# A selective-scan layer and an expert layer on one core: the delta stage keeps its exponentials in SBUF, in place, and gives the PSUM banks to products and projections

## The chip, the core and the metric

The kernel runs on one core of a Trainium2 chip. Time is the device time of one execution in microseconds (us), the median of several runs. The core's engines run side by side, each its own program in order: TensorE (PE, matrix products; PEld is its weight load), VectorE (DVE) and GpSimd (POOL) for element-wise work, ScalarE (ACT) for functions such as exp and log, and SyncE (SP), which here only issues DMAs. They wait for each other by semaphores. Products land in PSUM, which has eight banks of 128 partitions x 512 fp32; everything else lies in SBUF.

## What is computed

Two layers. In the first, the image x (2 x 256 x 48 x 48) is normalized and cut into 8 units (2 images x 4 branches of 64 channels). Each unit goes through this:

```python
x = silu(depthwise_conv3x3(x @ in_W) + conv_b)                  # 128 channels, L = 2304 positions
xs = stack([x, x_transposed, x[::-1], x_transposed[::-1]])      # K = 4 directions
dts, Bmat, Cmat = split(einsum('bkdl,kcd->bkcl', xs, x_proj_W)) # R = 4, N = 16, N = 16 rows
delta = softplus(einsum('bkrl,kdr->bkdl', dts, dt_W) + dt_b)
# scan over L: h = h * exp(delta * A) + (delta * u) * B ; y = sum_n h * C
```

then a norm, an output product and a skip. The second layer is an attention over all 4608 positions and a mixture of 8 experts. The part that matters here is softplus(v), which the kernel computes as max(v, 0) + log(1 + exp(-|v|)) with a correction for what is lost when 1 is added to the exponential.

## The kernel before

The program is a row of stages: setup, norm, delta, scan, mid (the join of the four directions, and the output product), attention, blend, gate, experts. Each stage ends before the next begins.

The delta stage writes delta and delta * u for the scan, and the rows B and C. Its loop has 16 groups: group g is unit g // 2 and the pair of directions g % 2, so 2 x 2304 = 4608 columns, cut into nine pieces (i = 0 to 8) of 512 columns. n = 9 g + i numbers the pieces. Each engine's program is written out by hand; its order is the order of the loops in the code:

- TensorE, per piece: `expand` (the product with dt_W in two matmuls, high and low part, into a bank of `ps_a`), in six of the nine pieces `project` (384 columns of the rows for the group to come, into `ps_b`), and half a block of the convolution for a unit to come (`convolve`, into `ps_c`). `expand` waits until the bank's last reader, the third VectorE operation, is done (`v_done`). `project` waits until the block before it has been taken out of `ps_b` (`lo_done`, `even_taken`).
- ScalarE, per piece: `magnitude(n + 1)`, the absolute value of the product, from `ps_a` to the SBUF buffer `mag`; then the exponential of piece n, from `mag` to a bank of `ps_e`, which waits until VectorE is done with that bank (`co_done`); then, where there is a projection, one or two copies out of `ps_b` (`take_block`). After nine pieces come three logarithms of 1536 columns each (`log`), in place in `du`, the third of which needs VectorE's second operation of piece 8. Exponentials after logarithms need a table load, and so do logarithms after exponentials. After the even groups a SiLU of the next unit follows (`silu`), but for the last unit.
- VectorE, per piece: first (L541) `du` = (e + 1) - 1, second (L545) `de` = e - `du`, third (L549) `de` = max(v, 0) + `de`, v still in `ps_a`. Between first and second stands `take_block`: a copy of 96 rows (every second block) and the low part of the rows to be cut. Between second and third stands, in pieces 1, 4 and 7, the copy of a convolution block out of `ps_c` (`take_conv`).
- GpSimd, after the logarithms of a group: six additions (`add_log`, L564) and six products (`drive`, L571) of 768 columns, alternately. After each even group it also makes the transposed image of the next unit (`turn`, L557).
- SyncE stores each part of 768 columns as it is done.

PSUM's eight banks are three for `ps_a`, two for `ps_e`, one for `ps_b`, two for `ps_c`.

Of the kernel before, what the change touches and what calls it, by code (L numbers as in the profile page):

```python
# [276 lines left out]
def delta_phase(nc, P, keep):  # L277
# [4 lines left out]
    with ExitStack() as ctx:  # L282
# [3 lines left out]
        xt = [s.sb(f"xt{i}", [128, L]) for i in range(2)]  # L286
        bc = [s.sb(f"bc{i}", [6 * N, L]) for i in range(2)]
        cut = [s.sb(f"cut{i}", [STACK, L], F32R) for i in range(2)]
        mag = [s.sb(f"mag{i}", [128, PIECE]) for i in range(3)]
        de = [s.sb(f"de{i}", [128, 2 * L]) for i in range(2)]  # L290
        du = [s.sb(f"du{i}", [128, 2 * L]) for i in range(2)]
        ps_a = [s.ps(f"ps_a{i}", [128, PIECE]) for i in range(3)]
        ps_e = [s.ps(f"ps_e{i}", [128, PIECE]) for i in range(2)]
        ps_b = s.ps("ps_b", [128, PIECE])
        ps_c = [s.ps(f"ps_c{i}", [128, PIECE]) for i in range(2)]
        cleared, ones_set, xs_ready, xt_ready = s.sem("cleared"), s.sem("ones_set"), s.sem("xs_ready"), s.sem("xt_ready")
        img_here = [s.sem(f"img_here{i}") for i in range(2)]
# [90 lines left out]
        @block.tensor  # L388
        def _(pe):
            def convolve(unit, t, first, last):  # L390
                o = ps_c[t % 2][:, 0:TT]
                ov = o.rearrange("p (r w) -> p r w", w=W)
                iv = img[unit % 2][:, :].rearrange("p (r w) -> p r w", w=W)
                r0 = t * (TT // W)
                RB = TT // W
                if first == 0:
                    if t == 0:
                        pe.wait_ge(img_here[unit % 2], 32 * (unit // 2) + 32)
                    if unit * TPI + t >= 2:
# [12 lines left out]

            def project(g, b):
                u, p = divmod(g, PAIRS)
                m = TPI * g + b
                if b == 0:
                    if p == 0:
                        pe.wait_ge(xs_ready, u + 1)
                    else:
                        pe.wait_ge(xt_ready, u + 1)  # L420
                if m:
                    pe.wait_ge(lo_done, m)
                    pe.wait_ge(even_taken, (m + 1) // 2)
                x = xs[u % 3] if p == 0 else xt[u % 2]
                pe.matmul(ps_b[:, 0:TT], keep["w_bc"][:, p, :], x[:, b * TT:b * TT + TT], start=True, stop=True).then_inc(b_full, 1)

            def expand(g, i):
                n = g * IG + i
                pe.wait_ge(hi_done, TPI * g + blocks_for(i))
                pe.wait_ge(lo_done, TPI * g + blocks_for(i))  # L430
                if n >= 3:
                    pe.wait_ge(v_done, n - 2)
                for r, at, a, b in spans(i):
                    d = g % PAIRS + 2 * r
                    pe.matmul(ps_a[n % 3][:, a:b], keep["w_dt"][:, d, :], cut[g % 2][:, at:at + b - a], start=True, stop=False)
                    mm = pe.matmul(ps_a[n % 3][:, a:b], keep["w_dt_lo"][:, d, :], cut[g % 2][:, at:at + b - a], start=False, stop=True)
                mm.then_inc(a_full, 1)

            for t in range(TPI):
                convolve(0, t, 0, 6)  # L440
            for t in range(3):
                convolve(1, t, 0, 6)
            pe.wait_ge(ones_set, 2)
            for b in range(TPI):
                project(0, b)
            for g in range(G):
                for i in range(IG):
                    expand(g, i)
                    if proj_block(g, i):
                        project(*proj_block(g, i))  # L450
                    if conv_block(g, i) and i % 3 < 2:
                        convolve(*conv_block(g, i), 3 * (i % 3), 3 * (i % 3) + 3)

        @block.scalar
        def _(act):
# [4 lines left out]
            def take_block(g, b):  # L460
# [3 lines left out]
                    act.wait_ge(bc_out[g % 2], 128 * (g // 2))  # L464
                    act.wait_ge(a_full, IG * (g - 1))
                if m % 2 == 0:
                    act.activation(bc[g % 2][:, b * TT:b * TT + TT], ps_b[0:6 * N, 0:TT], ACT.Copy).then_inc(even_taken, 1)
                act.activation(cut[g % 2][0:40, b * TT:b * TT + TT], ps_b[0:40, 0:TT], ACT.Copy).then_inc(hi_done, 1)

            def magnitude(n):  # L470
                act.wait_ge(a_full, n + 1)
                act.activation(mag[n % 3][:, :], ps_a[n % 3][:, :], ACT.Abs).then_inc(mag_done, 1)

            def log(g, r):
                act.wait_ge(co_done, IG * g + 3 * r + 3)
# [8 lines left out]
            for g in range(G):  # L484
                for i in range(IG):
# [1 line left out]
                    if n + 1 < G * IG:  # L487
                        magnitude(n + 1)
                    act.wait_ge(mag_done, n + 1)
                    if n >= 2:  # L490
                        act.wait_ge(co_done, n - 1)
                    act.activation(ps_e[n % 2][:, :], mag[n % 3][:, :], ACT.Exp, scale=-1.0).then_inc(ex_done, 1)
                    if i + 1 < IG and proj_block(g, i + 1):
                        take_block(*proj_block(g, i + 1))
                for r in range(LOGS):
# [5 lines left out]
        def _(dve):  # L501
# [8 lines left out]
            def take_block(g, b):  # L510
                m = TPI * g + b
                dve.wait_ge(hi_done, m + 1)
                if m % 2:
                    dve.tensor_copy(bc[g % 2][:, b * TT:b * TT + TT], ps_b[0:6 * N, 0:TT]).then_inc(odd_taken, 1)
                at = slice(b * TT, b * TT + TT)
                dve.tensor_tensor(cut[g % 2][64:104, at], ps_b[0:40, 0:TT], cut[g % 2][0:40, at].bitcast(F32), ALU.subtract).then_inc(lo_done, 1)

            for k in range(2):
                dve.memset(img[k][:, :], 0.0)
            for k in range(2):  # L520
                dve.memset(cut[k][64:STACK, :].bitcast(F32), 0.0)
                dve.memset(cut[k][32:64, :].bitcast(F32), 1.0).then_inc(ones_set, 1)
# [9 lines left out]
            for g in range(G):  # L532
                for i in range(IG):
# [16 lines left out]

        @block.gpsimd
        def _(pool):
# [1687 lines left out]
```

## Time and profile before

| | us |
|---|---|
| median of 3 runs | 5893.06 |
| lowest, highest | 5884.61, 5897.52 |
| the profiled execution | 5879.69 |
| its span, first to last instruction | 5877.3 |
| of it the delta stage's loop, 176 to 681 us | 505 |

The profile is of one execution. Its times count from the span's start. A row of the timeline says when an instruction started, how long it took, the engine, the line of the code, what it wrote from what it read, and in brackets how long its engine had stood idle before it and for whose result. Rows that follow each other directly on one engine are merged, with their number (x2). A group of the table by line has the number of instructions, their busy time and the mean of one, then the idle time of the engine just before them. Instructions on one engine overlap by about 0.1 us where they need nothing of each other, so their starts tell their pace better than their durations. Names are those of the code with the stage ahead: delta_ps_a is `ps_a` of the delta stage.

### The profile page before, as it was taken

To read this page: it belongs to the slowest core of one execution; us is meant where nothing else is said; L and a number is where in the kernel's file an instruction comes from. 1 tells how busy PE (TensorE), PEld (TensorE's weight loads), DVE (VectorE), ACT (ScalarE), POOL (GpSimd) and SP (SyncE) were. 2 spreads that over 40 slices of the span, in tenths; PEclk is the share of its full clock that TensorE was granted. 3 is DMA by queue.
4 is the path that set the end of the run, shared out by engine and by line. 5 is a ranking of instruction groups with operands and counts; after the bars stand their busy time and mean duration, and the time that the engine had idled before them with its cause. 6 is when DMAs were issued, how large, how long until landed. Compare 5 with 4: busy or idle time off the path is not lost. (4 is left out here: it accounts for less than half of the span.)

```text
span 5877.3 us, 82874 instructions
## 1 busy us (share of the span) xinstructions
PE 5051.9 (86%) x21540; PEld 3367.2 (57%) x21540; DVE 4209.1 (72%) x4029; ACT 3787.9 (64%) x8376; POOL 4259.4 (72%) x2720
## 2 busy tenths in 40 slices
PE   4777499999899898898898889995799999995997
PEld 2344255555555555555555555553458888884675
DVE  3677599999999999999999999996751111118334
ACT  2566588888888888888888888883442222226332
POOL 0576699999999999999999999995504444444442
PEclk8889599999999999999999999998999999996898
DMA  3676677777777777777777777775600000004113
GB/s 91 172 212 208 207 241 248 248 249 250 242 252 247 238 248 246 246 245 240 248 245 241 247 249 248 248 250 193 229 26 0 0 0 0 0 0 123 50 58 132
DMA packets 395504, 1045.37 MB, mean 178 GB/s; under 512 B 53422, under 2 KB 90319, under 8 KB 390944
## 3 DMA queue, kind: packets, MB, share of 16 engines
q1 hardware_dynamic: 380816, 1009.75, 53.0%
q0 software_dynamic: 7584, 20.72, 1.0%
q10 hardware_dynamic: 6640, 9.74, 0.4%
q8 instruction: 166, 2.72, 0.2%
q14 instruction: 298, 2.44, 0.1%
HBM read 869.23 MB, written 170.79 MB: 177 GB/s over the span
## 5 line engine op out<-in xcount | busy, mean ns | idle before, releaser
L909 POOL TENSOR_TENSOR scan_hc<-scan_h,scan_c_rep 128x768 f32<-128x768 f32 x1536 | 2749.3, 1822 | 227.3 <-PE scan_ps_y L740 180.2
L740 PE MATMUL scan_ps_y<-scan_hc,keep_ident 128*128 128x512 f32 (+1 forms) x6144 | 2217.6, 489 | 23.6 <-ACT scan_y L775 23.2
L874 DVE TENSOR_TENSOR_SCAN scan_h<-scan_da,scan_h,scan_ps_p 128x768 f32<-128x768 f32 x896 | 1568.6, 1796 | 0.0
L740 PEld LDWEIGHTS scan_ps_y<-scan_hc,keep_ident 128*128 128x128 f32 x6144 | 1066.6, 190 | 823.1 <-issue 738.1
L792 ACT ACTIVATE scan_warm<-scan_du_t 128x128 f32<-128x128 f32 x4608 | 1423.6, 388 | 35.8 <-PE scan_ps_p L731 30.2
L831 ACT ACTIVATE scan_da<-scan_dd,layer_a_neg 128x768 f32<-128x768 f32 x1344 | 1184.7, 922 | 6.1 <-issue 5.7
L1456 POOL TENSOR_TENSOR attn_e_lo<-attn_e,attn_e_hi 128x512 fp32r<-128x512 f32 x324 | 420.2, 1297 | 605.1 <-DVE attn_e_hi L1447 605.1
L731 PE MATMUL scan_ps_p<-keep_ident,scan_warm 128*128 128x128 f32 x4608 | 646.7, 277 | 224.2 <-DVE scan_h L874 223.4
L874 DVE TENSOR_TENSOR_SCAN scan_h<-scan_da,scan_ps_p 128x768 f32<-128x768 f32 x448 | 758.8, 1735 | 2.2 <-ACT scan_da L831 2.0
L731 PEld LDWEIGHTS scan_ps_p<-keep_ident,scan_warm 128*128 128x128 f32 x4608 | 531.9, 141 | 374.3 <-issue 157.0
L853 DVE TENSOR_TENSOR scan_ps_p<-scan_ps_p,scan_dd 128x768 f32<-128x768 f32 x576 | 547.5, 951 | 186.1 <-PE scan_ps_p L723 185.2
L1447 DVE CAST attn_e_hi<-attn_e 128x512 fp32r<-128x512 f32 x324 | 146.4, 452 | 721.5 <-ACT attn_e L1435 721.5
L1435 ACT ACTIVATE attn_e<-attn_ps_s 128x512 f32<-128x512 f32 x324 | 194.0, 599 | 705.8 <-PE attn_ps_s L74 705.8
L723 PE MATMUL scan_ps_p<-scan_cut,layer_b_sel 128*128 128x512 f32 (+1 forms) x1152 | 381.1, 412 | 56.9 <-DVE scan_h L874 48.7
L831 ACT ACTIVATE scan_ps_p<-scan_dd,layer_a_neg 128x768 f32<-128x768 f32 x192 | 172.2, 897 | 273.8 <-DVE scan_h L874 273.8
L903 POOL TENSOR_TENSOR scan_bu<-scan_dd,scan_b_rep 128x768 f32<-128x768 f32 x192 | 348.4, 1814 | 0.0
L564 POOL TENSOR_TENSOR delta_de<-delta_de,delta_du 128x768 f32<-128x768 f32 x96 | 173.5, 1814 | 182.5 <-ACT delta_du L477 182.5
L723 PEld LDWEIGHTS scan_ps_p<-scan_cut,layer_b_sel 128*128 128x128 f32 x1152 | 196.0, 190 | 155.9 <-DVE scan_h L874 134.6
L72 PE MATMUL attn_ps_o<-attn_e_hi,t_lo 128*128 128x512 f32 x648 | 259.6, 401 | 0.0
L72 PE MATMUL attn_ps_s<-f_hi,f_lo 128*128 x648 | 255.1, 394 | 2.1 <-DVE t_lo L1443 2.1
L74 PE MATMUL attn_ps_o<-attn_e_hi,t_hi 128*128 128x512 f32 x648 | 256.8, 396 | 0.0
L73 PE MATMUL attn_ps_s<-f_lo,f_hi 128*128 x648 | 255.8, 395 | 0.0
(328 smaller groups left out, 6869.4 us busy)
## 6 DMA issues: line engine op xcount, KB each, us to landing
scan_c_rep<-bc_dram SPq DMA_DIRECT2D x1536, 384.0 KB, 4.1
scan_dd<-dd_dram SPq DMA_DIRECT2D x96, 768.0 KB, 5.7
scan_b_rep<-bc_dram SPq DMA_DIRECT2D x192, 384.0 KB, 4.7
dd_dram<-delta_de SPq DMA_DIRECT2D x96, 384.0 KB, 2.6
dd_dram<-delta_du SPq DMA_DIRECT2D x96, 384.0 KB, 3.2
y_dram<-scan_y SPq DMA_DIRECT2D x96, 384.0 KB, 4.4
mid_nat<-y_dram SPq DMA_DIRECT2D x48, 384.0 KB, 5.3
delta_img<-xn_dram SPq DMA_DIRECT2D x16, 576.0 KB, 8.6
```

The costliest lines, as they stand in the source:

```text
L72: pe.matmul(out, wl, xh, start=start, stop=False)
L74: return pe.matmul(out, wh, xh, start=False, stop=stop)
L723: mm = pe.matmul(ps_p[place(t) % PR][:, lo:hi], keep["b_sel"][:, n, :], cut[st % 2][:, lo:hi], start=True, stop=True)
L731: mm = pe.transpose(ps_p[place(t) % PR][:, b * 128:b * 128 + 128], warm[w % WR][:, b, :], keep["ident"][:, :])
L740: mm = pe.matmul(ps_y[:, lo:hi], keep["ident"][:, :], hc[t % HR][:, lo:hi], start=n == 0, stop=n == N - 1)
L792: last = act.activation(warm[w % WR][:, b, :], du_t[st % 2][:, b * 128:b * 128 + 128], ACT.Identity, scale=du_t[st % 2][:, at:at + 1])
L831: act.activation(dst, dd[st % 2][:, 0, :], ACT.Exp, scale=keep["a_neg"][:, k, n:n + 1]).then_inc(ex_done, 1)
L853: dve.tensor_tensor(x, x, dd[st % 2][:, 1, :], ALU.mult).then_inc(mult_done, 1)
L874: dve.tensor_tensor_scan(view(h[n]), view(x), view(y), start, ALU.mult, ALU.add).then_inc(scan_done, 1)
L903: pool.tensor_tensor(bu[f % SR][:, :], dd[st % 2][:, 1, :], b_rep[f % SR][:, :], ALU.mult).then_inc(bu_done, 1)
L909: pool.tensor_tensor(hc[t % HR][:, :], h[t % N][:, :], c_rep[t % CR][:, :], ALU.mult).then_inc(hc_done, 1)
L1456: pool.tensor_tensor(e_lo[j % 3][:, :], e[j % 3][:, :], e_hi[j % 3][:, :].bitcast(F32), ALU.subtract).then_inc(lo_done, 1)
```

## The change

Three edits, all in the delta stage:

1. The exponential is written over its argument in `mag`, which has six buffers in place of three; `ps_e` is gone. `magnitude` waits for the buffer (`co_done`, six pieces back), the exponential waits for nothing but its argument. VectorE's first two operations read `mag`. The first becomes a `scalar_tensor_tensor`, whose second operand is a new column `less` of -1, broadcast over 512 columns.
2. The two banks go to a fourth buffer of `ps_a` and a second of `ps_b`. `expand` waits for the piece four back, `project` for the block two back.
3. `take_conv` stands in pieces 2, 5 and 8.

```diff
-        mag = [s.sb(f"mag{i}", [128, PIECE]) for i in range(3)]
+        MR, AR = 6, 4
+        mag = [s.sb(f"mag{i}", [128, PIECE]) for i in range(MR)]
+        less = s.sb("less", [128, 1])
...
-        ps_a = [s.ps(f"ps_a{i}", [128, PIECE]) for i in range(3)]
-        ps_e = [s.ps(f"ps_e{i}", [128, PIECE]) for i in range(2)]
-        ps_b = s.ps("ps_b", [128, PIECE])
+        ps_a = [s.ps(f"ps_a{i}", [128, PIECE]) for i in range(AR)]
+        ps_b = [s.ps(f"ps_b{i}", [128, PIECE]) for i in range(2)]
...
-                if m:
-                    pe.wait_ge(lo_done, m)
-                    pe.wait_ge(even_taken, (m + 1) // 2)
+                if m >= 2:
+                    pe.wait_ge(lo_done, m - 1)
+                    pe.wait_ge(even_taken, m // 2)
...
-                if n >= 3:
-                    pe.wait_ge(v_done, n - 2)
+                if n >= AR:
+                    pe.wait_ge(v_done, n - AR + 1)
...
-                act.activation(mag[n % 3][:, :], ps_a[n % 3][:, :], ACT.Abs).then_inc(mag_done, 1)
+                if n >= MR:
+                    act.wait_ge(co_done, n - MR + 1)
+                act.activation(mag[n % MR][:, :], ps_a[n % AR][:, :], ACT.Abs).then_inc(mag_done, 1)
...
-                    if n >= 2:
-                        act.wait_ge(co_done, n - 1)
-                    act.activation(ps_e[n % 2][:, :], mag[n % 3][:, :], ACT.Exp, scale=-1.0).then_inc(ex_done, 1)
+                    act.activation(mag[n % MR][:, :], mag[n % MR][:, :], ACT.Exp, scale=-1.0).then_inc(ex_done, 1)
...
+            dve.memset(less[:, :], -1.0)
...
-                    dve.tensor_scalar(du[g % 2][:, at], ps_e[n % 2][:, :], 1.0, -1.0, ALU.add, ALU.add).then_inc(dm_done, 1)
+                    dve.scalar_tensor_tensor(du[g % 2][:, at], mag[n % MR][:, :], 1.0, less[:, 0:1].to_broadcast([128, PIECE]), ALU.add, ALU.add).then_inc(dm_done, 1)
...
-                    dve.tensor_tensor(de[g % 2][:, at], ps_e[n % 2][:, :], du[g % 2][:, at], ALU.subtract).then_inc(co_done, 1)
-                    if conv_block(g, i) and i % 3 == 1:
+                    dve.tensor_tensor(de[g % 2][:, at], mag[n % MR][:, :], du[g % 2][:, at], ALU.subtract).then_inc(co_done, 1)
+                    if conv_block(g, i) and i % 3 == 2:
                         take_conv(*conv_block(g, i))
                     dve.wait_ge(co_done, n + 1)
-                    dve.scalar_tensor_tensor(de[g % 2][:, at], ps_a[n % 3][:, :], 0.0, de[g % 2][:, at], ALU.max, ALU.add).then_inc(v_done, 1)
+                    dve.scalar_tensor_tensor(de[g % 2][:, at], ps_a[n % AR][:, :], 0.0, de[g % 2][:, at], ALU.max, ALU.add).then_inc(v_done, 1)
```

VectorE at the end of the first group, pieces 7 and 8 and the first operation of the next group; before:

```order
L541 TENSOR_SCALAR delta_du0<-delta_ps_e1 128x512 [waits delta_ex_done]
L514 COPY delta_bc1<-delta_ps_b 96x384 [waits delta_hi_done]
L516 TENSOR_TENSOR delta_cut1<-delta_ps_b,delta_cut1 40x384
L545 TENSOR_TENSOR delta_de0<-delta_ps_e1,delta_du0 128x512 [waits delta_dm_done]
L508 COPY delta_xs1<-delta_ps_c1 128x384 [waits delta_c_full]
L549 SCALAR_TENSOR_TENSOR delta_de0<-delta_ps_a1,delta_de0 128x512 [waits delta_co_done]
L541 TENSOR_SCALAR delta_du0<-delta_ps_e0 128x512 [waits delta_ex_done]
L545 TENSOR_TENSOR delta_de0<-delta_ps_e0,delta_du0 128x512 [waits delta_dm_done]
L549 SCALAR_TENSOR_TENSOR delta_de0<-delta_ps_a2,delta_de0 128x512 [waits delta_co_done]
L541 TENSOR_SCALAR delta_du1<-delta_ps_e1 128x512 [waits delta_ex_done]
```

The same place now:

```order
L543 SCALAR_TENSOR_TENSOR delta_du0<-delta_mag1,delta_less 128x512 [waits delta_ex_done]
L515 COPY delta_bc1<-delta_ps_b1 96x384 [waits delta_hi_done]
L517 TENSOR_TENSOR delta_cut1<-delta_ps_b1,delta_cut1 40x384
L547 TENSOR_TENSOR delta_de0<-delta_mag1,delta_du0 128x512 [waits delta_dm_done]
L551 SCALAR_TENSOR_TENSOR delta_de0<-delta_ps_a3,delta_de0 128x512 [waits delta_co_done]
L543 SCALAR_TENSOR_TENSOR delta_du0<-delta_mag2,delta_less 128x512 [waits delta_ex_done]
L547 TENSOR_TENSOR delta_de0<-delta_mag2,delta_du0 128x512 [waits delta_dm_done]
L509 COPY delta_xs1<-delta_ps_c1 128x384 [waits delta_c_full]
L551 SCALAR_TENSOR_TENSOR delta_de0<-delta_ps_a0,delta_de0 128x512 [waits delta_co_done]
L543 SCALAR_TENSOR_TENSOR delta_du1<-delta_mag3,delta_less 128x512 [waits delta_ex_done]
```

The convolution copy moved from piece 7 to piece 8, behind the operation that counts up `co_done`; the first two operations of each piece have two operands in SBUF.

ScalarE at the same place, from the last block copy over the logarithms to the next group's first exponential; before:

```order
L468 ACTIVATE delta_cut1<-delta_ps_b 40x384 [waits delta_b_full]
L472 ACTIVATE delta_mag0<-delta_ps_a0 128x512 [waits delta_a_full]
L492 ACTIVATE delta_ps_e0<-delta_mag2 128x512 [waits delta_co_done,delta_mag_done]
L477 ACT_TABLE_LOAD
L477 ACTIVATE delta_du0<-delta_du0 128x1536 [waits delta_co_done] x3
L458 ACT_TABLE_LOAD
L458 ACTIVATE delta_xs1<-delta_xs1,layer0_conv_b 128x2304 [waits delta_c_taken]
L472 ACTIVATE delta_mag1<-delta_ps_a1 128x512 [waits delta_a_full]
L492 ACT_TABLE_LOAD [waits delta_co_done]
L492 ACTIVATE delta_ps_e1<-delta_mag0 128x512 [waits delta_mag_done]
```

And now:

```order
L469 ACTIVATE delta_cut1<-delta_ps_b1 40x384 [waits delta_b_full]
L475 ACTIVATE delta_mag3<-delta_ps_a1 128x512 [waits delta_co_done,delta_a_full]
L493 ACTIVATE delta_mag2<-delta_mag2 128x512 [waits delta_mag_done]
L480 ACT_TABLE_LOAD
L480 ACTIVATE delta_du0<-delta_du0 128x1536 [waits delta_co_done] x3
L459 ACT_TABLE_LOAD
L459 ACTIVATE delta_xs1<-delta_xs1,layer0_conv_b 128x2304 [waits delta_c_taken]
L475 ACTIVATE delta_mag4<-delta_ps_a2 128x512 [waits delta_co_done,delta_a_full]
L493 ACT_TABLE_LOAD
L493 ACTIVATE delta_mag3<-delta_mag3 128x512 [waits delta_mag_done]
```

The order of ScalarE's work is as it was; the wait for `co_done` moved from the exponential to the magnitude.

## Rows read from the trace of the kernel before

**Rows 1.** Windows: each engine's busy us (instructions), TensorE's clock, DMA share, GB/s

```profile
176.00:681.00 505.00, 341.21 (x950) 187.99 (x948) 378.63 (x606) 337.63 (x513) 349.84 (x188) 0.83 0.69 205
```

**Rows 2.** Groups by line, VectorE, 176 to 681 us: busy, mean ns | idle before, releasers

```profile
L545 DVE TENSOR_TENSOR delta_de<-delta_ps_e,delta_du 128x512 f32<-128x512 f32 x144 | 99.6, 692 | 4.7
...
L541 DVE TENSOR_SCALAR delta_du<-delta_ps_e 128x512 f32<-128x512 f32 x144 | 99.0, 687 | 116.4 <-ACT delta_ps_e L492 115.8
```

**Rows 3.** Waits, 176 to 681 us: us in total, times, longest

```profile
POOL delta_de L564 <- ACT delta_du L477: 182.5, 16, 51.7
```

**Rows 4.** Timeline around two group ends: start, us, engine, line [idle before]

```profile
393.27 4.23 ACT L477 ACTIVATE delta_du<-delta_du 128x1536 f32<-128x1536 f32 x3
...
403.53 0.69 DVE L541 TENSOR_SCALAR delta_du<-delta_ps_e 128x512 f32<-128x512 f32 x1 [7.70 <-ACT delta_ps_e L492]
...
423.29 0.69 DVE L549 SCALAR_TENSOR_TENSOR delta_de<-delta_ps_a,delta_de 128x512 f32<-128x512 f32 x1
...
424.26 0.69 DVE L541 TENSOR_SCALAR delta_du<-delta_ps_e 128x512 f32<-128x512 f32 x1 [0.28 <-ACT delta_ps_e L492]
...
424.87 0.54 DVE L514 COPY delta_bc<-delta_ps_b 96x384 f32<-96x384 f32 x1
...
426.03 0.69 DVE L545 TENSOR_TENSOR delta_de<-delta_ps_e,delta_du 128x512 f32<-128x512 f32 x1
...
427.10 0.68 DVE L549 SCALAR_TENSOR_TENSOR delta_de<-delta_ps_a,delta_de 128x512 f32<-128x512 f32 x1
427.26 4.23 ACT L477 ACTIVATE delta_du<-delta_du 128x1536 f32<-128x1536 f32 x3
427.70 0.68 DVE L541 TENSOR_SCALAR delta_du<-delta_ps_e 128x512 f32<-128x512 f32 x1
...
428.41 0.69 DVE L545 TENSOR_TENSOR delta_de<-delta_ps_e,delta_du 128x512 f32<-128x512 f32 x1
...
428.82 3.61 POOL L564 TENSOR_TENSOR delta_de<-delta_de,delta_du 128x768 f32<-128x768 f32 x2 [8.55 <-ACT delta_du L477]
...
432.38 1.81 POOL L571 TENSOR_TENSOR delta_du<-delta_de,delta_xt 128x768 f32<-128x768 f32 x1
...
433.99 0.69 DVE L541 TENSOR_SCALAR delta_du<-delta_ps_e 128x512 f32<-128x512 f32 x1 [4.16 <-ACT delta_ps_e L492]
...
458.11 4.23 ACT L477 ACTIVATE delta_du<-delta_du 128x1536 f32<-128x1536 f32 x3
```

**Rows 5.** Timeline in the mid stage, VectorE and GpSimd

```profile
4127.72 2.79 POOL L1030 TENSOR_TENSOR mid_q<-f_lo 128x768 f32<-128x768 f32 x1
4127.79 3.53 DVE L1269 SCALAR_TENSOR_TENSOR mid_a<-mid_nat,mid_d_sum,mid_a 128x768 f32<-128x768 f32 x1 [1.70 <-POOL mid_a L1025]
4130.47 2.52 POOL L1025 TENSOR_TENSOR mid_a<-mid_nat 128x768 f32<-128x768 f32 x1
4131.36 2.44 DVE L1273 TENSOR_TENSOR mid_a<-mid_a,mid_q 128x768 f32<-128x768 f32 x1
4132.95 3.51 POOL L1030 TENSOR_TENSOR mid_q<-f_lo 128x768 f32<-128x768 f32 x1
```

**Rows 6.** Timeline in the gate stage, VectorE and GpSimd

```profile
5415.19 2.61 POOL L1792 TENSOR_TENSOR keep_w_lo<-gate_raw,keep_w_hi 128x1024 fp32r<-128x1024 f32 x1 [2.21 <-ACT keep_w_hi L1821]
5415.52 3.10 DVE L1916 TENSOR_TENSOR gate_hot_r<-keep_iota,gate_rt 128x768 bf16<-128x768 f32 x1
```

**Rows 7.** Lines L239 and L243, norm stage: times, min/median/max ns, first and last start

```profile
L239 DVE TENSOR_TENSOR norm_xc<-norm_x,norm_ps_m x12: 953/954/955, 32.0 to 71.7; 128x768 f32<-128x768 f32 x12
...
L243 DVE TENSOR_TENSOR norm_xc<-norm_xc,norm_rs x12: 951/952/959, 47.4 to 84.8; 128x768 f32<-128x768 f32 x12
```

**Rows 8.** Line L557, delta stage

```profile
L557 POOL COPY delta_xt<-delta_xs x8: 4127/4179/4227, 144.5 to 610.6; 128x2304 f32<-128x2304 f32 x8
```

**Rows 9.** Timeline of the first group's row blocks, first projection and last cut

```profile
152.87 0.81 PE L425 MATMUL delta_ps_b<-delta_xs,layer_w_bc 128*128 128x384 f32 x2
...
170.13 0.55 DVE L516 TENSOR_TENSOR delta_cut<-delta_ps_b,delta_cut 40x384 fp32r<-40x384 f32 x1
```

More of the change, by code:

```diff
@@ L420, in project @@
                         pe.wait_ge(xt_ready, u + 1)
-                if m:
-                    pe.wait_ge(lo_done, m)
-                    pe.wait_ge(even_taken, (m + 1) // 2)
+                if m >= 2:
+                    pe.wait_ge(lo_done, m - 1)
+                    pe.wait_ge(even_taken, m // 2)
                 x = xs[u % 3] if p == 0 else xt[u % 2]
-                pe.matmul(ps_b[:, 0:TT], keep["w_bc"][:, p, :], x[:, b * TT:b * TT + TT], start=True, stop=True).then_inc(b_full, 1)
+                pe.matmul(ps_b[m % 2][:, 0:TT], keep["w_bc"][:, p, :], x[:, b * TT:b * TT + TT], start=True, stop=True).then_inc(b_full, 1)
             def expand(g, i):
@@ L430, in expand @@
                 pe.wait_ge(lo_done, TPI * g + blocks_for(i))
-                if n >= 3:
-                    pe.wait_ge(v_done, n - 2)
+                if n >= AR:
+                    pe.wait_ge(v_done, n - AR + 1)
                 for r, at, a, b in spans(i):
                     d = g % PAIRS + 2 * r
-                    pe.matmul(ps_a[n % 3][:, a:b], keep["w_dt"][:, d, :], cut[g % 2][:, at:at + b - a], start=True, stop=False)
-                    mm = pe.matmul(ps_a[n % 3][:, a:b], keep["w_dt_lo"][:, d, :], cut[g % 2][:, at:at + b - a], start=False, stop=True)
+                    pe.matmul(ps_a[n % AR][:, a:b], keep["w_dt"][:, d, :], cut[g % 2][:, at:at + b - a], start=True, stop=False)
+                    mm = pe.matmul(ps_a[n % AR][:, a:b], keep["w_dt_lo"][:, d, :], cut[g % 2][:, at:at + b - a], start=False, stop=True)
                 mm.then_inc(a_full, 1)
@@ L466, in take_block @@
                 if m % 2 == 0:
-                    act.activation(bc[g % 2][:, b * TT:b * TT + TT], ps_b[0:6 * N, 0:TT], ACT.Copy).then_inc(even_taken, 1)
-                act.activation(cut[g % 2][0:40, b * TT:b * TT + TT], ps_b[0:40, 0:TT], ACT.Copy).then_inc(hi_done, 1)
+                    act.activation(bc[g % 2][:, b * TT:b * TT + TT], ps_b[m % 2][0:6 * N, 0:TT], ACT.Copy).then_inc(even_taken, 1)
+                act.activation(cut[g % 2][0:40, b * TT:b * TT + TT], ps_b[m % 2][0:40, 0:TT], ACT.Copy).then_inc(hi_done, 1)
             def magnitude(n):
                 act.wait_ge(a_full, n + 1)
-                act.activation(mag[n % 3][:, :], ps_a[n % 3][:, :], ACT.Abs).then_inc(mag_done, 1)
+                if n >= MR:
+                    act.wait_ge(co_done, n - MR + 1)
+                act.activation(mag[n % MR][:, :], ps_a[n % AR][:, :], ACT.Abs).then_inc(mag_done, 1)
             def log(g, r):
@@ L513, in take_block @@
                 if m % 2:
-                    dve.tensor_copy(bc[g % 2][:, b * TT:b * TT + TT], ps_b[0:6 * N, 0:TT]).then_inc(odd_taken, 1)
+                    dve.tensor_copy(bc[g % 2][:, b * TT:b * TT + TT], ps_b[m % 2][0:6 * N, 0:TT]).then_inc(odd_taken, 1)
                 at = slice(b * TT, b * TT + TT)
-                dve.tensor_tensor(cut[g % 2][64:104, at], ps_b[0:40, 0:TT], cut[g % 2][0:40, at].bitcast(F32), ALU.subtract).then_inc(lo_done, 1)
+                dve.tensor_tensor(cut[g % 2][64:104, at], ps_b[m % 2][0:40, 0:TT], cut[g % 2][0:40, at].bitcast(F32), ALU.subtract).then_inc(lo_done, 1)
             for k in range(2):
                 dve.memset(img[k][:, :], 0.0)
+            dve.memset(less[:, :], -1.0)
             for k in range(2):
```

## The prediction

> **What bounds the kernel now.** I read the windows by stage first: the change touches only the delta stage, whose main loop is a stretch of 505 us in which VectorE works 379 us, GpSimd 350, TensorE 341 and ScalarE 338 [rows 1]. No engine is full, so the stage is a chain. The groups of VectorE's lines say where it breaks: 115.8 us of idle time stand in front of the first operation of a piece, until ScalarE's exponential [rows 2]. The timeline shows the shape of it [rows 4]. A group is nine pieces of 512 columns. At its end ScalarE does three logarithms with a table load before and after them, and then the first exponential of the next group; VectorE has finished its last piece and stands for 4.16 us, or 7.70 us where a SiLU comes in between as well. Two groups, one with the SiLU and one without, take 458.11 - 393.27 = 64.84 us. In between VectorE runs at its own pace, with 0.28 us lost now and then. GpSimd has its twelve operations of 1.8 us after each set of logarithms, and is idle 182.5 us in all, 51.7 of them before its first [rows 3]. So the stage is bound by VectorE plus the stand at each group's end, with GpSimd working beside VectorE for about 23 of each 32 us.
>
> **What the change gains.** Pieces of VectorE, from the starts in [rows 4]: first operation to second 0.71 us (427.70 to 428.41), each row copy or cut between them 0.58 (424.87 to 426.03 holds two) in front of a first operation that then takes 0.61; third operation to the next piece 0.60; second to third 0.72, or 1.07 with a convolution copy. So a piece costs 2.5 us with one block operation, 3.1 with two, 2.05 with none, and 0.35 more with the copy: 8.0 for three, as before and after, since the copy moves from the second piece of three to the third. The one change there is that the copy of piece 8 stands behind the operation that the logarithm waits for.
> Fourth product buffer: before, the logarithms start at 427.26, 3.28 us after the third operation of piece 6 ends (423.29 + 0.69); that is the expansion for the next group, its magnitude, the exponential of piece 8 and the table load. With four buffers and exponentials that need no bank, the same chain hangs on piece 5. Counted from the start of piece 6 (time 0), the logarithms then start at 0.1 + 3.3 = 3.4. Two logarithms end at 6.3; the third needs the second operation of piece 8, which without any disturbance starts at 2.5 + 3.1 + 0.7 = 6.3 and ends at 7.0. The third logarithm ends at 8.5. From the end of the logarithms to the next group's first operation the rows give 433.99 - 431.49 = 2.5 us, and 403.53 - 397.50 = 6.0 us with the SiLU: 11.0 and 14.5. Six more pieces of 16.0 together: 27.0 and 30.5, with some 0.8 of TensorE's delay behind the SiLU left in, 58.4 us for two groups where there were 64.8. Over seven such pairs and one more boundary that is about 47 us.
> Second projection bank: the first six row blocks take from 152.87 to 170.68 [rows 9], one after another, since each projection waits for the cut of the block before it. Two banks let two blocks overlap; of nearly 3 us a block I take 1.5 off for four of them: 6 us (0 to 8). In the loop projections are not late, so nothing there.
> New memset, one column: nothing. ScalarE writes SBUF in place of PSUM: ScalarE has at least 2 us to spare per piece once VectorE is late; nothing, and at the group's end one exponential, within 0.1 us a group either way.
> VectorE's sources: SBUF in place of PSUM. The same form of 768 columns took 954 ns with one PSUM source and 952 ns with two SBUF sources [rows 7], GpSimd idle both times: nothing. The Trainium skill ("VectorE: DVE Perf Modes", the section on the TRN2 errata) has 58 cycles for SBUF and 120 for PSUM; that would be 62 cycles less, an estimate of 0.065 us for each of 288 operations, 19 us. The rows don't show it, and it is not in the sum.
>
> **What the change costs.** It gives two of VectorE's three operations per piece two SBUF inputs: the first now reads the exponentials and a broadcast column, the second the exponentials and the result of the first. Before, each had one input in PSUM, and with GpSimd beside them they kept to 692 and 687 ns [rows 2]. The trace has VectorE operations with two SBUF inputs beside GpSimd in the stage that joins the scans [rows 5]. At 4127.79 such an operation of 768 columns takes 3.53 us; GpSimd's began at 4127.72 and ended at 4130.51, and VectorE's ends 0.81 later. GpSimd's next took 2.52, not 1.81, and VectorE's next ends again 0.8 after it (4131.36 + 2.44 = 4133.80). So it is one after the other: VectorE's operation waits for the whole GpSimd operation, then goes first, and GpSimd's next is put off by 0.71. A broadcast operand does not help: in [rows 6] an operation whose second operand is a broadcast takes 3.10 us, until 0.82 after GpSimd's end at 5417.80.
> The Trainium skill says so too ("SBUF — State Buffer", Who interferes with whom): a VectorE instruction with two SBUF inputs contends with a GpSimd one that reads SBUF, and the later of the two is blocked for all of it. By that rule, the trace agrees, in every pair in [rows 5].
> For 512 columns I take 0.26 us off, the difference between 954 ns for 768 columns [rows 7] and 692 ns for 512 [rows 2]: VectorE's operation ends 0.55 after GpSimd's, and GpSimd is put off 0.45. GpSimd alone has a cadence of 1.77 ((432.38 - 428.82) / 2). So under GpSimd one of these operations goes through per 1.77 + 0.45 = 2.22 us. What VectorE does between them (0.6 to 1.3 us) fits into that; a piece takes 4.4 us for 2.7. The walk, from the start of piece 6:
> GpSimd starts 1.56 after the logarithms (428.82 - 427.26), at 5.0. The first operation of piece 8 asks at 5.6, waits for 6.8, ends 7.3; the second waits for GpSimd's next, until 9.0, and ends 9.55 in place of 7.0. Third logarithm until 11.0; next group at 13.5, or 17.05 with the SiLU. GpSimd's operations 3 to 7 run at 1.77 from 9.4 on and end at 11.2, 13.0, 14.7, 16.5, 18.3.
> Without SiLU: blocked operations go at the ends of GpSimd's 5 to 12, the first at 14.7 and the last at 14.7 + 7 x 2.22 = 30.2. These are eight, so four pieces; piece 4 starts at 31.4, and 3.1 + 2.4 later piece 6: 36.9.
> With SiLU: operations 7 to 12 carry six, 18.3 to 29.4; then GpSimd's turn, a copy of 4.18 us [rows 8], holds the first operation of piece 3 until 34.0, and piece 6 starts at 41.9. Before, the pair was 64.84; now 78.8: 14.0 more. Seven pairs are 98, the one odd boundary 6.5: +104. The gains of the first part are inside the walk. Less 6 for the first blocks: **+98 us**.
> The profiled execution took 5879.7 us (span 5877.3 and 2.4 around it): 5977.7. The median of the runs stands 13.4 above it, so I forecast **5990**.
> Where I chose: that the turn blocks like the two-input operations is not in the rows; without it the seven SiLU groups lose 2.9 us less, 20 in all. The first blocked operation of piece 8 is only 0.6 us later than GpSimd's start; were it earlier, 1.2 us a group go, 17 in all. And 0.1 us on each of about 140 blocked operations is 14. Together with the 0 to 8 us of the first blocks these give 5945 to 6010.
>
> **Rivals.**
> (a) Nothing blocks: the broadcast and the in-place buffers are read as PSUM was. Then the first part stands alone, -47 and -6: **5840**, faster. It speaks for it that [rows 2] show both lines at an even 690 ns beside GpSimd; against it that there each has only one SBUF input, and that [rows 5, 6] show the wait for both forms. It would decide from a wait below a third of what I take: the gain is 53, the blocking costs 151. 7 in 100.
> (b) Only the second operation blocks, the broadcast being free. The same walk, with one blocked operation a piece: 30.4 and 36.2, pair 66.6, +12 over seven pairs, less 6: **5900**, the same. Against it [rows 6]. 5 in 100.
> (c) GpSimd does not give way after each operation, or not always. Then VectorE's pieces come nearly all after GpSimd's: 5 + 12 x 1.77 + six pieces of 16 us is 42 to 43 for 36.9 without the SiLU, +6 per group: **6080**. Against it the alternation in [rows 5], where VectorE goes first at every end of a GpSimd operation. 6 in 100.
> (d) The blocking is as walked, but the stand behind it grows, since the stores or TensorE come late by it: up to 6040. Part of the main case's range.
>
> **How the numbers follow.** The walk has 82 in 100, of which 4 lie below 5945 or above 6040; (a) 7, (b) 5, (c) 6. The range 5945 to 6040 holds about 8 in 10. A measurement here tells 0.2%, 12 us. Faster is (a): 0.07. Same: (b), 0.05. Slower: 0.88.
>
> **What the profile after would show.** Right: the two lines that write delta_du and delta_de from delta_mag have a minimum near 690 ns and a mean well above, 1.3 to 1.5 us, with maxima near 2.4 and 4.7; the third, with its PSUM input, stays at 690; GpSimd's adds and products rise from 1.81 to a mean near 2.1; two groups take near 79 us from logarithm to logarithm. The idle time before the first operation of a piece falls below 80 us, and the stage is slower all the same. The scan and later stages don't change. Wrong: both lines at 690 and pairs of 58 us (a); the first line at 690 alone (b); single waits of several GpSimd operations (c). If the pair is 79 but the total isn't, a later stage gave or took it.

## The result, and the profile after

The changed kernel takes 5983.74 us (median of 4 runs, 5979.22 to 5989.98), the kernel before 5895.29 us (5884.61 to 5898.23): a ratio of 1.0151, 95% interval 1.0133 to 1.0169, so 88 us slower (78 to 100). The profiled execution took 5984.46 us, its span is 5982.6.

The windows by stage: each engine's busy us (instructions), TensorE's clock, DMA share, GB/s. This is the loop of the delta stage after; [rows 1] answer to it.

```profile
165.00:774.00 609.00, 365.83 (x951) 203.09 (x950) 526.54 (x604) 338.74 (x513) 406.25 (x188) 0.77 0.58 170
```

The loop takes 609 us where it took 505, for nearly the same instructions (604 of VectorE's for 606). VectorE's busy time grew from 379 to 527 us, GpSimd's from 350 to 406; ScalarE's did not move. The groups by line in the delta stage after, VectorE and GpSimd: shape, count | busy us, mean ns | idle before, releaser. [Rows 2] answer to the first two.

```profile
L543 DVE SCALAR_TENSOR_TENSOR delta_du<-delta_mag,delta_less 128x512 f32<-128x512 f32 x144 | 182.6, 1268 | 74.8 <-ACT delta_mag L493 74.8
L547 DVE TENSOR_TENSOR delta_de<-delta_mag,delta_du 128x512 f32<-128x512 f32 x144 | 174.7, 1213 | 4.7
L551 DVE SCALAR_TENSOR_TENSOR delta_de<-delta_ps_a,delta_de 128x512 f32<-128x512 f32 x144 | 99.0, 688 | 3.6
```

```profile
L566 POOL TENSOR_TENSOR delta_de<-delta_de,delta_du 128x768 f32<-128x768 f32 x96 | 197.3, 2062 | 219.2 <-ACT delta_du L480 219.2
L573 POOL TENSOR_TENSOR delta_du<-delta_de,delta_xt 128x768 f32<-128x768 f32 x48 | 102.7, 2147 | 0.0
```

The two operations that now have both inputs in SBUF went from 687 and 692 ns to 1268 and 1213; the third, which reads PSUM and SBUF as before, is at 688. The idle time in front of a piece fell from 115.8 us to 74.8, as the change meant it to, and the stage is slower all the same. The blocked time stands in the rows as busy time, not as a wait: (1268 - 687 + 1213 - 692) ns x 144 = 159 us.

The timeline at the group end with a SiLU that begins at 422.61, VectorE, GpSimd and ScalarE: start, us, engine, line.

```profile
422.61 2.86 ACT L480 ACTIVATE delta_du<-delta_du 128x1536 f32<-128x1536 f32 x2
...
424.17 4.02 POOL L566 TENSOR_TENSOR delta_de<-delta_de,delta_du 128x768 f32<-128x768 f32 x2 [11.63 <-ACT delta_du L480]
...
424.94 1.59 DVE L543 SCALAR_TENSOR_TENSOR delta_du<-delta_mag,delta_less 128x512 f32<-128x512 f32 x1
...
426.56 2.17 DVE L547 TENSOR_TENSOR delta_de<-delta_mag,delta_du 128x512 f32<-128x512 f32 x1
...
428.77 1.48 ACT L480 ACTIVATE delta_du<-delta_du 128x1536 f32<-128x1536 f32 x1 [3.30 <-DVE delta_de L547]
...
436.31 1.70 DVE L543 SCALAR_TENSOR_TENSOR delta_du<-delta_mag,delta_less 128x512 f32<-128x512 f32 x1 [6.51 <-ACT delta_mag L493]
...
446.96 2.17 DVE L547 TENSOR_TENSOR delta_de<-delta_mag,delta_du 128x512 f32<-128x512 f32 x1
...
448.54 4.63 POOL L559 COPY delta_xt<-delta_xs 128x2304 f32<-128x2304 f32 x1
...
450.13 3.59 DVE L543 SCALAR_TENSOR_TENSOR delta_du<-delta_mag,delta_less 128x512 f32<-128x512 f32 x1
...
455.67 0.68 DVE L543 SCALAR_TENSOR_TENSOR delta_du<-delta_mag,delta_less 128x512 f32<-128x512 f32 x1
```

Both operations of piece 8 wait for one GpSimd operation each (1.59 and 2.17 us in place of 0.69), and the third logarithm waits 3.30 us for the second of them. At 450.13 VectorE waits for the whole of GpSimd's transposing copy. As soon as GpSimd is through, the operation takes 0.68 us again (455.67). The first logarithms after, at the two ends of one pair of groups and between its two groups; [rows 4] hold the pair of before:

```profile
264.04 2.86 ACT L480 ACTIVATE delta_du<-delta_du 128x1536 f32<-128x1536 f32 x2
...
305.99 2.86 ACT L480 ACTIVATE delta_du<-delta_du 128x1536 f32<-128x1536 f32 x2
...
342.96 2.86 ACT L480 ACTIVATE delta_du<-delta_du 128x1536 f32<-128x1536 f32 x2
```

78.9 us for two groups, where it was 64.84: 42.0 for the one with the SiLU and 37.0 for the one without. The scan's first instruction on VectorE comes at 815.1 us, 95.4 later than before; the rest of the program differs by 10 us between the two profiled executions, and over the profiled executions of all kernels here the scan's stretch varies by 16 us without a pattern.

### The profile page after: what moved, and what is told of

The parts are those of the page before. It is cut to its first block and busy times, and to the rows that moved or that the text cites. A ratio compares the mean times of both kernels' runs of the same rounds, so it can differ in the third digit from the quotient of the medians.

```text
span 5982.6 us, 82870 instructions
## 1 busy us (share of the span) xinstructions
PE 5076.2 (85%) x21540; PEld 3384.3 (57%) x21540; DVE 4364.9 (73%) x4030; ACT 3788.8 (63%) x8376; POOL 4319.2 (72%) x2720
## 5 line engine op out<-in xcount | busy, mean ns | idle before, releaser
L566 POOL TENSOR_TENSOR delta_de<-delta_de,delta_du 128x768 f32<-128x768 f32 x96 | 197.3, 2062 | 219.2 <-ACT delta_du L480 219.2
```

## The experiments

Each ratio is to runs of the kernel before on the same chip.

**1. Both operations with a PSUM input.** Everything as changed, but the operands are where GpSimd's reads don't meet them. The formula is another (maxima for sums), so only the time is read.

```diff
-  dve.scalar_tensor_tensor(du[..], mag[n % MR][:, :], 1.0, less[:, 0:1].to_broadcast([128, PIECE]), ALU.add, ALU.add)
+  dve.scalar_tensor_tensor(du[..], mag[n % MR][:, :], 1.0, ps_a[n % AR][:, :], ALU.add, ALU.max)
-  dve.tensor_tensor(de[..], mag[n % MR][:, :], du[..], ALU.subtract)
+  dve.tensor_tensor(de[..], ps_a[n % AR][:, :], du[..], ALU.max)
```

> The changed kernel, but the first two operations of VectorE's piece read the product bank ps_a in place of the column of -1 and in place of the exponentials, so that each has one SBUF input; buffers, waits and GpSimd's work are as changed (the formula is another: maxima in place of the sums). Theory (blocking behind GpSimd): both operations go back to an even 690 ns, GpSimd to 1.81 us, two groups take near 58.4 us from logarithm to logarithm, the total is near 5838 us (before 5895, less 47 for the groups and the 10.6 us by which the first group began earlier in the changed kernel). Rival (the slowdown comes from the buffers, the waits or ScalarE's writes to SBUF): two groups stay at 79 us and the total near 5984.

Measured: 5832.92 us, ratio 0.9902 (0.9874 to 0.9929). The groups by line of this kernel:

```profile
L547 DVE TENSOR_TENSOR delta_de<-delta_ps_a,delta_du 128x512 f32<-128x512 f32 x144 | 99.6, 692 | 4.7
L551 DVE SCALAR_TENSOR_TENSOR delta_de<-delta_ps_a,delta_de 128x512 f32<-128x512 f32 x144 | 99.2, 689 | 3.6
L543 DVE SCALAR_TENSOR_TENSOR delta_du<-delta_mag,delta_ps_a 128x512 f32<-128x512 f32 x144 | 97.8, 679 | 82.3 <-ACT delta_mag L493 82.3
```

Both are back at 690 ns, with GpSimd's additions at 1818 ns, and two groups take 59.2 to 60.3 us. So the whole loss is where the operands lie: 151 us between this kernel and the changed one. The rest of the change (the banks, the buffers, the moved copy) gains 61 us by the medians. Between the profiled executions it is 51, since that of before was one of the fastest of its kernel (see experiments 9 and 10).

**2 and 3. One operation at a time.** Only the first line of the diff above (with a maximum in the second operation), then only the second; what is computed differs in both, the work doesn't.

> The changed kernel, but only the first operation of the piece has a PSUM operand (ps_a for the column of -1, the formula is another); the second still has two SBUF inputs. Theory (each operation with two SBUF inputs waits for the GpSimd operation that runs): one blocked operation a piece, two groups near 66.6 us by the walk of the prediction's rival (b), the total near 5897; the first line at 690 ns, the second well above. Rival (only the broadcast column blocks): near 5838.

> The changed kernel, but only the second operation has a PSUM operand (ps_a for the exponentials, the formula is another); the first still reads the exponentials and the broadcast column from SBUF. Theory: a broadcast column is a second SBUF input like any other, so one blocked operation a piece, two groups 64 to 68 us, the total 5885 to 5905. Rival (the broadcast is free): near 5838.

Measured: 5897.88 us, ratio 1.0013 (1.0000 to 1.0027), with the second operation blocked (mean 1212 ns), and 5924.55 us, ratio 1.0055 (1.0037 to 1.0072), with the first (mean 1342 ns). The broadcast column does block. The pairs take 68.4 and mostly 71.9 us where I had 66.6 and 64 to 68. The total of the first came out as expected (near 5897); that of the second, expected at 5885 to 5905, was missed by 20 us. The timeline of experiment 3, first operation and GpSimd, shows why:

```profile
377.34 2.27 POOL L573 TENSOR_TENSOR delta_du<-delta_de,delta_xt 128x768 f32<-128x768 f32 x1
...
379.58 1.81 POOL L566 TENSOR_TENSOR delta_de<-delta_de,delta_du 128x768 f32<-128x768 f32 x1
...
379.89 2.05 DVE L543 SCALAR_TENSOR_TENSOR delta_du<-delta_mag,delta_less 128x512 f32<-128x512 f32 x1
...
381.35 2.25 POOL L573 TENSOR_TENSOR delta_du<-delta_de,delta_xt 128x768 f32<-128x768 f32 x1
...
383.57 1.81 POOL L566 TENSOR_TENSOR delta_de<-delta_de,delta_du 128x768 f32<-128x768 f32 x1
...
384.35 1.59 DVE L543 SCALAR_TENSOR_TENSOR delta_du<-delta_mag,delta_less 128x512 f32<-128x512 f32 x1
...
385.35 2.25 POOL L573 TENSOR_TENSOR delta_du<-delta_de,delta_xt 128x768 f32<-128x768 f32 x1
```

A piece falls into step with GpSimd. With one blocked operation it takes two of GpSimd's operations, 4.0 us (377.34, 381.35, 385.35), for the 2.7 that it needs; with two blocked ones it takes two as well, 4.4 us. So beside a running GpSimd the second blocked operation of a piece costs little more, and taking one away gives back 0.4 of 1.7 us. In experiment 2 the step is looser: the third operations of three pieces in a row start at 371.19, 375.18 and 377.75 us, and the next at 381.42, so that one piece in three slips through and a piece takes 3.4 us. The two kernels, each with one blocked operation, differ by 27 us in the same direction.

**4. The exponentials in place, and nothing else.** Three banks for ps_a and one for ps_b as before, the copy where it was; MR = 6 and the two operations as changed (the diff of the change without its lines on ps_a, ps_b and the copy; the two banks of ps_e lie idle).

> The kernel before, with the exponentials in place in six SBUF buffers and the first two operations as changed, but three banks for ps_a, one for ps_b, the convolution copy where it was. Theory (blocking alone): the logarithms start 3.3 us after piece 6, so both operations of piece 8 go before GpSimd begins; then ten and eight blocked operations a group; two groups 78 us, the total near 5990, so that the fourth bank and the moved copy together give about nothing while VectorE is blocked. Rival (the buffers hurt): near 5895.

Measured: 6013.16 us, ratio 1.0202 (1.0173 to 1.0230), slower even than the changed kernel by 29 us; 23 us above what I expected. The pair takes 81.9 us (363.43 to 445.32), not 78. The mechanism is the one that was expected: at this group end both operations of piece 8 go at 0.68 and 0.69 us, before GpSimd begins or just as it does, and later ones wait:

```profile
445.32 4.23 ACT L480 ACTIVATE delta_du<-delta_du 128x1536 f32<-128x1536 f32 x3
...
445.74 0.68 DVE L543 SCALAR_TENSOR_TENSOR delta_du<-delta_mag,delta_less 128x512 f32<-128x512 f32 x1
...
446.45 0.69 DVE L547 TENSOR_TENSOR delta_de<-delta_mag,delta_du 128x512 f32<-128x512 f32 x1
...
446.88 3.69 POOL L566 TENSOR_TENSOR delta_de<-delta_de,delta_du 128x768 f32<-128x768 f32 x2 [13.09 <-ACT delta_du L480]
```

So the other edits gave back 29 us of what the in-place exponentials cost: about 12 at the start (the first piece comes at 177.64 here and at 165.36 in the changed kernel) and 3 a pair. I had them at about nothing. Of the 2 us a group beyond my walk the trace shows half: once a pair VectorE stands 1.98 us (at 404.31) for an exponential behind a late expansion, a wait that the changed kernel doesn't have. TensorE's granted clock was 0.50, its lower level of 1.2 GHz, from 399 to 402 us, just before it. The other half stays open.

**5 and 6. GpSimd's operations cut to 8 of 768 columns,** in the changed kernel and in the kernel before.

```diff
+  at = slice(j * WC, j * WC + 8)
   pool.tensor_tensor(de[g % 2][:, at], de[g % 2][:, at], du[g % 2][:, at], ALU.add)
```

(and the same for the product; VectorE's second operation takes a maximum. Most of the sums and products are left out.)

> The changed kernel, but each of GpSimd's additions and products covers 8 columns in place of 768, so GpSimd is idle beside VectorE except for its turns; both VectorE operations keep two SBUF inputs (the second takes a maximum, and most of the sums are left out). Theory (blocking needs a long GpSimd operation): both lines at 690 ns except where a turn runs, two groups near 60 us, and 20 us less in the last group's tail: near 5830 us. Rival (two SBUF inputs are slow in themselves, or by the stores): near 5960.

> The kernel before with the same short GpSimd operations (most sums and products left out). Theory: nothing in the loop of before waits for GpSimd, so only the tail behind the last logarithms is shorter: two groups stay at 64.85 us, near 5874 us. Rival (VectorE's one-input operations are held up a little by GpSimd as well): below 5865 with a shorter pair.

Measured: 5826.52 us, ratio 0.9880 (0.9860 to 0.9900), and 5884.25 us, ratio 0.9978 (0.9964 to 0.9992). The changed kernel becomes 157 us faster when the other engine falls silent, the kernel before 9. Those 9 fit the shorter tail behind the last logarithms: from there to the scan's first instruction it is 31.2 us for 41.6. So some 10 of the 157 are tail as well. I had 20 for the tail; the stores behind it stay. I had expected pairs of 64.85 us in the kernel before. They take 63.8 to 68.1 (398.40 to 465.11 is 66.7), with VectorE's operations at 687 and 692 ns; experiments 9 and 10 come back to this. In the changed kernel the second operation is at 693 ns and the first at 757: seven of its 144 took longer than 0.75 us, each beside a transposing copy.

**7. The first operation as tensor_scalar.** In the changed kernel, the form of before with its source in SBUF.

```diff
-  dve.scalar_tensor_tensor(du[..], mag[n % MR][:, :], 1.0, less[:, 0:1].to_broadcast([128, PIECE]), ALU.add, ALU.add)
+  dve.tensor_scalar(du[..], mag[n % MR][:, :], 1.0, -1.0, ALU.add, ALU.add)
```

> The changed kernel with the first operation as tensor_scalar on SBUF, the form it had before, in place of the sum with the broadcast column. Theory: it runs faster where nothing blocks, 0.43 us for 512 columns as the cast in the attention stage does, but it waits for GpSimd's operations like the other: two groups near 74 us, the total near 5950. Rival (without a second operand it doesn't wait): two groups near 66, total near 5880.

Measured: 5946.02 us, ratio 1.0086 (1.0064 to 1.0109); the pair takes 75.2 us in five of seven cases (406.49 to 481.73; 73.7 and 74.7 in the others), where I had 74. The line, minimum, median, maximum in ns, and it beside the transposing copy:

```profile
L543 DVE TENSOR_SCALAR delta_du<-delta_mag x144: 415/956/3682, 164.0 to 740.7; 128x512 f32<-128x512 f32 x144
...
357.69 4.64 POOL L559 COPY delta_xt<-delta_xs 128x2304 f32<-128x2304 f32 x1
...
359.28 3.33 DVE L543 TENSOR_SCALAR delta_du<-delta_mag 128x512 f32<-128x512 f32 x1
```

It takes 415 ns where GpSimd is idle and waits for GpSimd where it is not (at 359.28 until 0.28 us after the copy's end), with one SBUF operand. The same form with its source in PSUM kept to 687 ns beside GpSimd in the kernel before. So a single SBUF operand is enough in this form, which takes 415 ns where the others take 680 and 692. It is still 38 us better than the broadcast column, so the new form was the worse of the two for SBUF.

**8. The form alone.** The kernel before with the sum and the broadcast column, exponentials in PSUM.

> The kernel before with only the form of the first operation changed: the sum with a broadcast column of -1, the exponentials still in PSUM, so one SBUF input. Theory: no blocking, the first line at 685 to 692 ns also beside GpSimd, the total within 3 us of before. Rival (this form or the broadcast column is slow in itself beside GpSimd): over 20 us more.

Measured: 5895.50 us, ratio 1.0003 (0.9994 to 1.0012). A broadcast column in SBUF beside a PSUM operand costs nothing: it is then the only SBUF input.

**9 and 10. The copy moved, and a bank lent.** The kernel before with `i % 3 == 2` in front of `take_conv`; then this with

```diff
+        def rows_at(m):
+            return ps_e[1] if m < TPI and m % 2 else ps_b
...
-                if m:
+                if 2 <= m <= TPI:
+                    pe.wait_ge(lo_done, m - 1)
+                    pe.wait_ge(even_taken, m // 2)
+                elif m > TPI:
                     pe.wait_ge(lo_done, m)
                     pe.wait_ge(even_taken, (m + 1) // 2)
...
+                    if n == 1:
+                        act.wait_ge(lo_done, TPI)
```

and `rows_at(m)` wherever ps_b stood: the first group's projections use two banks, since the exponentials don't need theirs yet.

> The kernel before with the convolution copy behind pieces 2, 5 and 8 alone. Theory: at a group's end ScalarE's chain hangs on the third operation of piece 6, with two copies ahead of it in either order, so the move is worth nothing: within 3 us of before. Rival (VectorE's second operation of piece 8 sets the third logarithm): 0.35 us a group, 5 us less.

> The kernel before with the convolution copy moved and the first group's odd row blocks in a bank of ps_e that is idle until the first exponentials. Theory: the second projection bank pays only in the first group, 10.6 us, and a lent bank gives it without the exponentials leaving PSUM: near 5884 us. Rival (the first group's gain came with the fourth product bank): near 5894.

Measured: 5882.91 us, ratio 0.9983 (0.9974 to 0.9991), and 5869.37 us, ratio 0.9963 (0.9950 to 0.9976). The second is a version that beats both kernels, 24 us under the one before. The bank's share is 13 us, near the 10.6 expected; the first operation of the first piece comes at 163.94 for 175.93 [rows 9 are of that stretch]:

```profile
163.94 0.69 DVE L550 TENSOR_SCALAR delta_du<-delta_ps_e 128x512 f32<-128x512 f32 x1 [3.73 <-ACT delta_ps_e L501]
```

The copy's share, 11 us, I did not expect from either theory. The pair in its profile is 64.8 us as in the profile of before, and the scan begins only 3.7 us earlier. But the profiled execution of before, 5879.7 us, was one of the fastest of that kernel, whose median is 5893, while this kernel's profiled one stands at its median. Experiment 8's kernel, with operations of the same durations and the median of before, shows pairs of 65.1 to 67.6 us. Its first logarithms, at the two ends of a pair of 66.8:

```profile
397.68 4.23 ACT L478 ACTIVATE delta_du<-delta_du 128x1536 f32<-128x1536 f32 x3
...
464.52 4.23 ACT L478 ACTIVATE delta_du<-delta_du 128x1536 f32<-128x1536 f32 x3
```

The traces show where these 2 us lie. VectorE's first operation of the second piece after a SiLU, and the windows from TensorE's first product after it (each engine's busy us and instructions, TensorE's clock, DMA share, GB/s); the kernel before, then experiment 8:

```profile
407.04 0.69 DVE L541 TENSOR_SCALAR delta_du<-delta_ps_e 128x512 f32<-128x512 f32 x1 [0.79 <-ACT delta_ps_e L492]
401.00:404.00 3.00, 2.92 (x5) 1.74 (x6) 0.47 (x1) 2.97 (x6) 3.00 (x3) 0.50 0.78 298
404.00:411.00 7.00, 5.31 (x18) 3.00 (x18) 6.05 (x11) 2.65 (x6) 7.00 (x5) 0.99 0.99 223
...
412.81 0.69 DVE L543 SCALAR_TENSOR_TENSOR delta_du<-delta_ps_e,delta_less 128x512 f32<-128x512 f32 x1 [2.15 <-ACT delta_ps_e L493]
405.40:411.00 5.60, 5.51 (x9) 3.17 (x10) 2.63 (x4) 3.18 (x6) 5.60 (x4) 0.50 0.88 275
411.00:415.40 4.40, 3.61 (x12) 1.98 (x11) 2.53 (x5) 2.45 (x5) 4.40 (x4) 0.97 1.00 215
```

TensorE stood idle for 6.4 us before both. In the kernel before its granted clock is at the lower level (0.50, 1.2 GHz) for 3 us more and then at the upper (2.4 GHz). In experiment 8 it stays at the lower for 5.6 us, so that the expansion is late, and with it the magnitude, the exponential and VectorE: 2.15 us for 0.79. In the group without a SiLU it is 1.76 us for 1.02: counted from the start of the logarithms before it, the clock is back at the upper level after 15.8 us in experiment 8 and after 14.3 in the kernel before. With the copy moved (this kernel's own profile) the stretch behind the SiLU is as bad as in experiment 8, 2.13 us of waiting, but in the other group the clock is back after 12.8 us and VectorE waits 0.24. So in these traces the moved copy saves a wait that the usual execution of before has and its profiled one mostly hasn't. That the usual one looks like experiment 8 is inferred from the times; and why the clock comes back sooner in one execution than in another was not tried.

**11. One activation table.** Experiment 10 with the table set that holds both exp and ln loaded ahead, so that most of the stage's 32 loads for exponentials and logarithms go. What it computes is not quite the same, so its time is read as an answer about ScalarE's chain, not as a kernel to use.

```diff
             magnitude(0)
+            act.preload_act_table_set(LOG_EXP)
             for g in range(G):
+                if g and g % PAIRS == 1:
+                    act.preload_act_table_set(LOG_EXP)
```

> The kernel before with three things that leave every VectorE operation with one SBUF input: the convolution copy moved as in the change, the first group's odd row blocks in a bank of ps_e that is still idle then, and one activation table that holds both the exponential and the logarithm, loaded once per SiLU, so that 1.28 us go before the logarithms and 1.28 us behind them where no SiLU stands. Theory: 10.6 us less at the start, about 2.2 us less at a group end without a SiLU and 0.9 with one, near 5862 us. Rival (the third logarithm hangs on VectorE's second operation of piece 8 at 429.1 us in the rows of before, so the earlier start is waited away): near 5880.

Measured: 5835.79 us, ratio 0.9904 (0.9888 to 0.9919). The pairs are 58.5 to 60.9 us (302.30 to 360.80 is 58.5), some 5 less, of which the loads are 3 x 1.28 = 3.8. So the rival falls, and my 3.1 a pair was too low; what gives the rest was not followed. The third logarithm doesn't wait: the three stand in one row of 4.22 us.

## Why the prediction was right

The forecast was 5990 us, the measured time is 5983.7, and the way there was the one forecast. By its steps:

- **Two SBUF inputs wait for GpSimd.** Right, and shown from both sides: moving the operands to PSUM (experiment 1) and silencing GpSimd (experiment 5) take away 151 and 157 us, the latter with some 10 of shorter tail. Rival (a) falls with it. The price of a blocked operation read in the mid stage [rows 5] carried over: 2.17 us for an operation that asks as GpSimd's begins, 1.59 us for one behind a piece's third operation, and GpSimd's median at 2.25 us against 1.81. No wait was longer than one GpSimd operation, so rival (c) falls too. Over 0.75 us took 145 of the 288 operations, where the forecast had about 140.
- **The walk.** The pair came out at 78.9 us against 78.8, its groups at 42.0 and 37.0 against 41.9 and 36.9, with the third logarithm's wait of 3.3 us at the place and the turn's blocking of 3.59 us, both of which had been steps. The one step that had no row, that the transposing copy blocks, is now a row (450.13). The signs were set a little high: means of 1.27 and 1.21 us for 1.3 to 1.5, a maximum of 3.92 for 4.7.
- **The first blocks.** 6 us forecast, 10.6 measured (first piece at 165.4 for 175.9). I had taken 1.5 us off for each of four blocks. The six blocks, from the first projection to the last cut, take 8.8 us (152.76 to 161.59) for 17.8, which is 1.8 us less for each of five; the other 1.5 us lie between the last cut and the first operation, 3.8 us for 5.3.
- **The gain without blocking.** 53 us forecast, worked out from the profile of before. Against that profile the scan of experiment 1 begins 53.4 us earlier, though the two terms come out otherwise: 42 us in the groups for 47 (most pairs 59.2 to 60.3 against 58.4), and 12 before the first logarithms for 6. By the medians it is 61.
- **PSUM and SBUF sources alike** in VectorE's own time: means of 678 to 693 ns in all kernels where nothing holds the operation up. By the Trainium skill ("VectorE: DVE Perf Modes", the TRN2 errata) an SBUF source has a smaller fixed part, and the first two lines would be near 625 ns, an estimate. No run here shows it: their shortest operations in the changed kernel took 680 and 692 ns. It was rightly left out of the sum.
- **The sum against the median.** The profiled execution of before was 13 us below its median, that of after at its own. Up to the scan the program grew by 95 us between the profiles, in all it grew by 105, and the medians by 88. That the forecast of the total met so well is partly luck: it added 98 to the median of before, while the profile that the 98 were worked out from had the shorter waits for TensorE (experiments 9 and 10).
- **Rival (b)** is the one whose price was furthest off: one blocked operation a piece was to cost a pair 1.7 us more than before; it cost 3.5 with the second operation blocked and 7 with the first. Its walk took the operations one by one and did not see that a piece falls into GpSimd's step, wholly or in part, for as long as GpSimd runs. Of the 151 us, giving the first operation alone its PSUM operand won 86 and the second alone 59.

## What to carry to other kernels

Before an operand moves from PSUM to SBUF, count the SBUF inputs of the VectorE operation that reads it and look at what GpSimd does at that time: with two inputs, a broadcast column among them, or with one in the form that took 415 ns for 512 columns, VectorE and GpSimd took turns here by whole instructions. The blocked time is booked as busy time, so the idle time can fall while the stage gets slower; a wide gap between the least and the mean duration of one form is the sign. A spare bank that is wanted only at the start can be lent from a buffer that isn't in use yet.

## What was not expected of the hardware

- With the first operation of a piece alone blocked, the loop falls into step with two GpSimd operations (4.0 us for 2.7), nearly the 4.4 us of two blocked operations; with the second alone it was 3.4 us.
- `tensor_scalar` with a single SBUF operand, 415 ns at its fastest, was held up to 3.68 us behind GpSimd.
- The loop of before shows pairs of 64.8 us in one execution and, with the same durations of VectorE's operations, 65 to 68 us in the traces of experiments 6 and 8. The difference shown is how long TensorE's granted clock stays at 0.50 after an idle stretch of the same 6.4 us: 3 us in one, 5.6 in the other.
